# Second attention: TensorE instead of VectorE adds up head 1's exponentials, and the scores use two PSUM banks

## The reference

```python
xn = layernorm(x)
x = x + attention0(xn) + ternary_mlp(xn)      # 32 query heads, 8 key/value heads, rotary, causal
xn = layernorm(x)
x = x + gated_cumsum(xn) + attention1(xn)     # 16 heads of width 32, causal
```

```python
scores = einsum('bhtd,bhsd->bhts', Qf, Kf) / sqrt(32)
scores = where(causal, scores, finfo.min)
attn = softmax(scores, axis=-1)
out = einsum('bhts,bhsd->bhtd', attn, V)      # 16 heads
y = out.transpose(0, 2, 1, 3).reshape(B, T, 512) @ Wp
```

## Time and profile before

| | us |
|---|---|
| runs: median (lowest to highest) of 3 | 2744.94 (2737.44 to 2747.92) |
| profiled execution: span from first to last instruction | 2700.3 |
| PE busy, share of the span | 2390.0, 89% |
| PEld busy | 1489.7, 55% |
| DVE busy | 1759.7, 65% |
| ACT busy | 1250.1, 46% |
| POOL busy | 511.4, 19% |
| second attention: first exponential at, last at | 2008.9, 2596.2 |

### The profile page before, as it was taken

One profiled execution on the slowest core, in us unless ns is written; L12 is line 12 of the kernel. 1 busy time (PEld: TensorE's weight loads), 2 busy tenths in 40 slices (PEclk: granted clock), 3 DMA queues, 4 the chain that ended last, 5 costly groups with the idle time before them and its releaser, 6 DMA issues. The chain is left out here.

```text
span 2700.3 us, 42116 instructions
## 1 busy us (share of the span) xinstructions
PE 2390.0 (89%) x16373; PEld 1489.7 (55%) x16373; DVE 1759.7 (65%) x2057; ACT 1250.1 (46%) x2357; POOL 511.4 (19%) x447
## 2 busy tenths in 40 slices
PE   4959999959999999999999479979969999999947
PEld 2758888835444444444444457758745555555515
DVE  3745444537888888888880343422259999999954
ACT  2422222202777877877876121212215555556531
POOL 1110000010000000000000002220036676667650
PEclk8979999958999999999999789989979999999978
DMA  3771000060221221220000510015562222220024
GB/s 124 236 230 47 32 31 31 0 78 14 36 39 24 42 39 24 43 39 18 10 9 4 143 63 0 1 47 117 192 145 48 48 65 65 65 63 10 8 67 143
DMA packets 121390, 164.67 MB, mean 61 GB/s; under 512 B 60848, under 2 KB 66608, under 8 KB 115824
## 3 DMA queue, kind: packets, MB, share of 16 engines
q1 hardware_dynamic: 117744, 149.52, 22.8%
q10 hardware_dynamic: 3456, 12.58, 1.4%
HBM read 114.19 MB, written 47.71 MB: 60 GB/s over the span
## 5 line engine op out<-in xcount | busy, mean ns | idle before, releaser
L615 ACT ACTIVATE a_ex<-a_ps_s 128x512 f32<-128x512 f32 (+3 forms) x1280 | 622.8, 532 | 296.9 <-PE a_ps_s L670 220.4
L770 DVE TENSOR_REDUCE a_mx_part<-a_ps 128x2 f32<-128x1024 f32 (+3 forms) x576 | 585.8, 1043 | 132.5 <-PE a_ps L635 130.3
L1042 ACT ACTIVATE a_ex<-a_ps_s 128x512 f32<-128x512 f32 (+3 forms) x640 | 318.4, 532 | 286.1 <-PE a_ps_s L1103 159.8
L670 PE MATMUL a_ps_s<-a_q,a_k 50*128 50x512 f32 (+3 forms) x1152 | 399.8, 416 | 0.0
L635 PE MATMUL a_ps<-a_k,a_q 48*128 48x512 f32 (+3 forms) x1152 | 353.2, 419 | 33.0 <-DMA a_q<-q 29.2
L1017 POOL TENSOR_TENSOR a_acc<-a_acc,a_ex 128x512 f32<-128x512 f32 (+3 forms) x288 | 351.6, 1221 | 96.5 <-ACT a_ex L1042 75.6
L713 PE MATMUL a_ps_o<-a_ex,a_v 128*32 128x256 f32 (+1 forms) x5120 | 359.8, 363 | 5.9 <-ACT a_o L603 5.4
L1167 DVE TENSOR_REDUCE a_mx_part<-a_ps 128x2 f32<-128x1024 f32 (+2 forms) x320 | 336.3, 1054 | 34.6 <-PE a_ps L1069 22.8
L670 PEld LDWEIGHTS a_ps_s<-a_q,a_k 50*128 50x128 f32 x1152 | 182.8, 187 | 209.1 <-ACT a_ex L615 140.9
L1670 POOL TENSOR_TENSOR gc_z<-gc_state,gc_qg 128x512 f32<-128x512 f32 x16 | 26.3, 1641 | 1197.8 <-DVE gc_qg L1658 1197.8
L1066 PE MATMUL a_ps<-a_k,a_q 96*128 96x512 f32 (+3 forms) x640 | 212.6, 399 | 43.7 <-DMA a_q<-q 22.9
(11 more groups left out here) (202 smaller groups left out, 3894.7 us busy)
## 6 DMA issues: line engine op xcount, KB each, us to landing
a_q<-q SPq DMA_DIRECT2D x48, 256.0 KB, 5.4
a_k<-k SPq DMA_DIRECT2D x24, 512.0 KB, 4.9
a_q<-q SPq DMA_DIRECT2D x24, 512.0 KB, 6.9
q<-p_oh SPq DMA_DIRECT2D x32, 256.0 KB, 2.5
q<-p_ol SPq DMA_DIRECT2D x32, 256.0 KB, 2.8
w_o<-o SPq DMA_DIRECT2D x8, 1024.0 KB
w_z<-z SPq DMA_DIRECT2D x32, 256.0 KB
a_k<-k SPq DMA_DIRECT2D x48, 128.0 KB, 3.4
```

The costliest lines, as they stand in the source:

```text
L615: act.activation(ex[unit % NE][:, h % 2, off:CH], ps_s[n % 3][:, off:CH], ACT.Exp, scale=SCALE)\
L670: pe.matmul(ps_s[n % 3][:, off:CH], k_st[st][r0:r0 + KM, h % KH, t * P:(t + 1) * P], q_st[st][r0:r0 + KM, slot_h, c * CH + off:(c + 1) * C ...
L770: dve.tensor_reduce(mx_part[:, 2 * p:2 * p + 2, i, kc], bank[:, :, 0:w], AX.X, ALU.max).then_inc(taken1, 1)
L1042: act.activation(ex[s % NE][:, h, off:CH], ps_s[n % 3][:, off:CH], ACT.Exp, scale=SCALE)\
```

## The change

In the second attention VectorE no longer adds head 1's exponentials. TensorE does: `add_up(b, half)` takes a block of four steps and multiplies each step's head 1 tile with `first_one`, a 128x32 weight with ones in its first column. The four steps go to four column groups of 32, so their sums over the keys stand side by side in the bank `ps_z` (partitions 0, 32, 64 and 96), accumulated over a chunk's blocks. A block is done in two halves of 256 columns, in the even steps that follow it, behind `scores(s, 1)`. In a group's first chunk a 512-wide product with zeros opens the bank. At a chunk's end ScalarE copies the bank to `spread` (`take_spread`), and the product with ones in `sums` adds the four partial sums as it did the 128 partitions of `acc` before.

The bank for `ps_z` comes from the scores: they have two banks in place of three, one for each head, so `scores(s, h)` waits for the exponential of step s - 1 of its own head. The ring `ex` is released by GpSimd's additions, `times_v` and `add_up`. Head 0's way is as before. VectorE's memsets at the start are five instead of two, and TensorE waits for them.

Apart from this, `project0` gives its 38 semaphores back after `ternary_mlp`, and SyncE clears them at the start of `ternary_mlp`, ahead of its weight loads.

```diff
-        acc = [[sb(f"acc{i}_{n}", [P, CH]) for n in range(HG)] for i in range(2)]
-        one = sb("one", [P, DH])
+        acc = [sb(f"acc{i}", [P, CH]) for i in range(2)]
+        spread = [sb(f"spread{i}", [P, CH]) for i in range(2)]
+        one, first_one = sb("one", [P, DH]), sb("first_one", [P, DH])
+        zero = sb("zero", [P, CH], F32R)
...
-        ps_s = [psum(f"ps_s{i}", [P, CH]) for i in range(3)]
+        ps_s = [psum(f"ps_s{h}", [P, CH]) for h in range(HG)]
         ps_o = psum("ps_o", [P, CH])
+        ps_z = psum("ps_z", [P, CH])
...
+            def take_spread(g, c, s):
+
+                j = g * NCH + c
+                act.wait_ge(summed, 2 * (s // TPC + 1))
+                if j >= 2:
+                    act.wait_ge(scores1, SUMS_ENTRY[j - 2] + 1)
+                act.activation(spread[j % 2][:, :], ps_z[:, :], ACT.Copy).then_inc(spread_done, 1)
+
...
                     if h == 0 and s >= NE:
                         act.wait_ge(pv_done, (s - NE) // 2 + 1)
-                        act.wait_ge(added0, s - NE + 1)
-                        act.wait_ge(added1, s - NE + 1)
-                    act.activation(ex[s % NE][:, h, off:CH], ps_s[n % 3][:, off:CH], ACT.Exp, scale=SCALE)\
+                        act.wait_ge(added, s - NE + 1)
+                        act.wait_ge(summed, 2 * ((s - NE) // TPC + 1))
+                    act.activation(ex[s % NE][:, h, off:CH], ps_s[h][:, off:CH], ACT.Exp, scale=SCALE)\
                         .then_inc(exp_done, 1)
+                    if h == 0 and s - 4 in LAST_STEP:
+                        take_spread(*LAST_STEP[s - 4], s - 4)
...
-                pe.wait_ge(added0, s + 1)
-                pe.wait_ge(added1, s + 1)
-                for h in range(HG):
-                    mm = pe.matmul(ps_1[m % 2][h * DH:(h + 1) * DH, 0, :], one[:, :], acc[j % 2][h][:, :],
+                pe.wait_ge(added, s + 1)
+                pe.wait_ge(spread_done, j + 1)
+                for h, total in enumerate((acc[j % 2], spread[j % 2])):
+                    mm = pe.matmul(ps_1[m % 2][h * DH:(h + 1) * DH, 0, :], one[:, :], total[:, :],
                                    start=True, stop=True)
...
-                if n >= 3:
-                    pe.wait_ge(exp_done, n - 2)
+                if s > 0:
+                    pe.wait_ge(exp_done, n - HG + 1)
...
+            def add_up(b, half):
+
+                g, c, t0 = STEP_LIST[TPC * b]
+                pe.wait_ge(exp_done, TPC * (b + 1) * HG)
+                if t0 == 0 and half == 0:
+                    if b > 0:
+                        pe.wait_ge(spread_done, g * NCH + c)
+                    if c == 0:
+                        pe.matmul(ps_z[:, :], sel[:, 0, :], zero[:, :], start=True, stop=False)
+                for j in range(TPC):
+                    s = TPC * b + j
+                    off = max(first_col(c, t0 + j), half * CH // 2)
+                    cols = slice(off, (half + 1) * CH // 2)
+                    if cols.start < cols.stop:
+                        mm = pe.matmul(ps_z[j * DH:(j + 1) * DH, cols], first_one[:, :], ex[s % NE][:, 1, cols],
+                                       start=c > 0 and t0 == 0 and half == 0, stop=t0 == TPC * c and half == 1)
+                mm.then_inc(summed, 1)
+
...
             pe.wait_ge(blank, NS)
+            pe.wait_ge(part_init, 5)
...
                 if s % 2 == 1 and s > 1:
                     times_v(s // 2 - 1)
+                if s % TPC == 0 and s >= TPC:
+                    add_up(s // TPC - 1, 0)
+                if s % TPC == 2 and s > TPC:
+                    add_up(s // TPC - 1, 1)
             times_v(len(STEP_LIST) // 2 - 1)
+            for half in range(2):
+                add_up(len(STEP_LIST) // TPC - 1, half)
...
-                if 0 <= s - 2 < len(STEP_LIST):
-                    add_ex(s - 2)
...
         def _(sp):
+            for s in done_with:
+                sp.sem_clear(s)
```

More of the change, by code:

```diff
@@ L116, with project0 @@
 LN_SEMS = ("mean", "centred", "squared", "var", "root", "inverse", "scaled", "high", "low")
-def project0(nc, keep, A, X, xh, xl, ones_mean, eps, D):
+def project0(nc, keep, done_with, A, X, xh, xl, ones_mean, eps, D):
     with ExitStack() as ctx:
@@ L129, in sem @@
         def sem(n):
-            return keep.enter_context(nc.semaphore(f"p0_{n}"))
+            done_with.append(keep.enter_context(nc.semaphore(f"p0_{n}")))
+            return done_with[-1]
         COLS = QK0 + P
@@ L892, in attention_two @@
         scores2, exp_done, pv_done = sem("scores2"), sem("exp_done"), sem("pv_done")
-        added0, added1 = sem("added0"), sem("added1")
+        added, summed, spread_done = sem("added0"), sem("added1"), sem("spread_done")
         taken_o, staged = sem("taken_o"), sem("staged")
@@ L1008, in _ @@
                 j, off = g * NCH + c, first_col(c, t)
-                total, tile = acc[j % 2][0], ex[s % NE][:, 0, off:CH]
+                total, tile = acc[j % 2], ex[s % NE][:, 0, off:CH]
                 pool.wait_ge(exp_done, s * HG + 1)
@@ L1013, in _ @@
                         pool.wait_ge(scores1, SUMS_ENTRY[j - 2] + 1)
-                    pool.tensor_copy(total[:, :], tile).then_inc(added0, 1)
+                    pool.tensor_copy(total[:, :], tile).then_inc(added, 1)
                 else:
-                    pool.wait_ge(added0, s)
-                    pool.tensor_tensor(total[:, off:CH], total[:, off:CH], tile, ALU.add).then_inc(added0, 1)
+                    pool.wait_ge(added, s)
+                    pool.tensor_tensor(total[:, off:CH], total[:, off:CH], tile, ALU.add).then_inc(added, 1)
             join(GROUPS - 1, NCH - 1)
@@ L1047, in _ @@
                 take_o(GROUPS - 1, NCH - 1, len(STEP_LIST) // 2 - 1, odd)
+            take_spread(GROUPS - 1, NCH - 1, len(STEP_LIST) - 1)
         @block.tensor
@@ L1096, in scores @@
                 off = first_col(c, t)
-                if n >= 3:
-                    pe.wait_ge(exp_done, n - 2)
+                if s > 0:
+                    pe.wait_ge(exp_done, n - HG + 1)
                 diagonal = t >= TPC * c
-                mm = pe.matmul(ps_s[n % 3][:, off:CH], k_st[st][0:KM, h, t * P:(t + 1) * P],
+                mm = pe.matmul(ps_s[h][:, off:CH], k_st[st][0:KM, h, t * P:(t + 1) * P],
                                q_st[st][0:KM, h, c * CH + off:(c + 1) * CH], start=True, stop=not diagonal)
                 if diagonal:
-                    mm = pe.matmul(ps_s[n % 3][:, off:off + P], sel[:, 0, :], low_k[:, :], start=False, stop=True)
+                    mm = pe.matmul(ps_s[h][:, off:off + P], sel[:, 0, :], low_k[:, :], start=False, stop=True)
                 mm.then_inc(scores2, 1)
@@ L1158, in _ @@
             dve.memset(one[:, :], 1.0).then_inc(part_init, 1)
-            dve.wait_ge(part_init, 2)
+            dve.memset(first_one[:, :], 0.0).then_inc(part_init, 1)
+            dve.memset(zero[:, :].bitcast(F32), 0.0).then_inc(part_init, 1)
+            dve.wait_ge(part_init, 4)
+            dve.memset(first_one[:, 0:1], 1.0).then_inc(part_init, 1)
             def maxima(n):
@@ L1914, in build @@
             xl = inner.enter_context(nc.sbuf_tensor("xl0", [P, KT, TOK], F32R))
-            project0(nc, keep, A, X, xh, xl, ones_mean, eps, D)
-            ternary_mlp(nc, keep, A, X, xh, xl, ones_mean, D)
+            with ExitStack() as projecting:
+                done_with = []
+                project0(nc, projecting, done_with, A, X, xh, xl, ones_mean, eps, D)
+                ternary_mlp(nc, keep, done_with, A, X, xh, xl, ones_mean, D)
         attention(nc, shared, "a0", ATTN0, D, 0, neg_ident, masks[2])
```

14 lines of the change are left out of this document (1 added, 13 removed).

## The result

The changed kernel takes 2797.43 us (median of 4 runs; 2795.36 to 2862.66) against 2741.19 (2717.8 to 2747.92) of the kernel before on the same chip: ratio 1.0239 [1.0185, 1.0293]. The highest run, a disturbed one, is left out of the ratio. The two sets of medians differ by 56 and 65 us, so the change costs some 60 us, where the forecast had 33.

The account below looks back on a forecast made before the run. VectorE was the bound, TensorE close behind. Groups +40.7, with -3, -4 and +2.1, gave +36, less 3 made +33 us: 2733 on the 2700.3 us span, 2778 us with 44.6 up to the median; range 2742 to 2820.

Parts of the forecast that it names:

- groups at clock 1.00: Second attention: 296 steps, or 7.4 groups of 40 steps, each 5.5 us longer, +40.7 us.
- widths "rounded up": Diagonal steps of the second attention: product widths were said to be rounded up, so 3 us were taken off.
- granted clock: Second attention: a TensorE without gaps should keep 2.4 GHz, -4 us, chosen between 0 and -6.
- last 24 steps: Second attention's last steps: no maxima and room enough on TensorE, so no cost counted.
- end of the stage: Last sums of the second attention: less waiting for VectorE's additions, but two halves and a copy come in, -3 us.
- TensorE's own work before: Second attention, per group: 64.7 us summed from spacings, against 74.0 measured, leaving 9.3 us of room.
- 20 halves and the zero product: TensorE's added work per group: 20 x 0.66 us plus one 512-wide zero product of 0.23, 13.4 us.
- waits at a chunk's end: TensorE's value product waiting for ScalarE's output-bank copy, formerly partly in its room, now paid: 1.4 us a group.
- 0.1 us twice: TensorE in the second attention: 0.1 us each on the way into and out of the 32-column products.
- second rival: Two score banks bind: exponentials 0.25 us late in half of the steps, 37 us more, 2815 us; chance 0.20.
- Cheap halves: TensorE's halves cost only 0.40 to 0.46 us: +2 us, 2747 us, no change; chance 0.18.
- Real room in TensorE: Spacings hide TensorE idle time in the second attention: some 90 us less, 2655 us, half of that 2700; chance 0.12.

Follow-up runs that it names:

- e6: Kernel before with VectorE's additions for head 1 left out and nothing in their place, so head 1's sums are missing: 2683.72 us, ratio 0.9859.
- e3: Changed kernel with each half replaced by one 128-wide product, head 1's sums left out: 2721.64 us, ratio 1.0001.
- e5: Kernel before with only the change's two score banks, VectorE's additions kept: 2739.61 us against 2735.51.
- e1: The changed kernel run again without edit, beside the kernel before: 2784.35 us against 2718.91, ratio 1.0239.
- e4: Changed kernel with the halves moved behind the value products in the odd steps, bank copy one step later: 2786.62 us.
- e7: Changed kernel with one 512-wide sum per block of four steps in place of two halves: 2778.5 us, ratio 1.0226.
- e2: Kernel before with only the 38 semaphore clears ahead of the MLP's weight loads: 2734.25 us, ratio 0.9993.
- e8: Kernel before with the semaphore clears; GpSimd takes head 1's additions of each group's second chunk from VectorE: 2789.62 us.
- e9: Kernel before with the semaphore clears; GpSimd takes head 1's additions of each group's first chunk from VectorE: 2747.44 us, ratio 1.007.
- e10: Kernel before with the semaphore clears; GpSimd takes head 1's additions of every chunk's two narrowest steps from VectorE: 2746.11 us, ratio 1.0087.

## Why the prediction came out as it did

Direction and mechanism were right for the steady groups: VectorE stopped being the bound, TensorE's room was used up, and its column products set the step. The size was not. The measured 2797.43 us lies inside the wide range (2742 to 2820) and just above the forecast's own (2762 to 2795), and the cost was nearly twice the 33 us. By terms of the stage, in us:

| | predicted | measured |
|---|---|---|
| groups at clock 1.00 | 7.4 x 5.5 = +40.7 | 7.4 x 9.2 = +68 |
| widths "rounded up" | -3 | nothing: they were too small |
| granted clock | -4 | some -10 |
| last 24 steps | 0 | +6.5 |
| end of the stage | -3 | -4.5 |
| sum | +31 | +60 (stage: +59) |

The larger part lies in the first line, and there in one sum. For a group:

| | predicted | measured |
|---|---|---|
| TensorE's own work before | 64.7 | 68.5 (e6: 70.4 less 1.9 of waits) |
| 20 halves and the zero product | 13.4 | 20 x 0.77 + 0.2 = 15.6 |
| waits at a chunk's end | 1.4 | none that PE's gaps show |
| sum | 79.5 | 84.1; the group takes 83.3 |

*Own work, the step that failed.* "9.3 us of room" was 74.1 less 70.4, some 4. The 36.7 us of the twelve pairs off the diagonal rest on a stretch read directly; short were the terms that were scaled or counted. First, the diagonal's widths: with its mask a 384-wide product costs 0.04 us more than the prediction said and a 512-wide one behind a mask 0.05, and four passes (two heads, scores and maxima) in four chunks make 16 x 0.09 = 1.4 us. Second, the diagonal's 5.5 us a chunk has two value products, yet "0.1 us twice" once (2 x 1.87 + 0.99 + 0.55 + 0.2). The trace of after shows both paying on the way in and out there (0.16 us from a mask to L1136 instead of 0.06, and 0.22 for the 256-wide score behind it instead of 0.12), which is 0.2 us a chunk, 0.8 a group. Third, a flip was counted at its record of 0.38 us; with 0.1 us in, 0.31 and 0.1 us out it costs 0.51, 0.5 us a group. That is 2.7 of the 3.8 us; the rest was not found row by row and may hold short waits. The prediction then took off 3 us because its widths were "rounded up". They were too small, so that correction had the wrong sign.

*A half: 0.66 predicted, 0.77 measured.* The 0.56 us of the records and the 0.1 us on the way in were right. The 0.1 us behind it was missed, although show it: 0.35 us from the score after L1120 to the next product. The rule "0.1 us twice" was read off the value product and then applied once to the half. The Trainium skill, "TensorE: Matmul & The Clock Gate", section "Measured speedup vs the span model", gave an estimate of 0.40 us; the trace of after disagrees, as that of before had for the value product, with 0.56 us to the next start.

*The waits at a chunk's end* went the other way. Before, the value product's group was

```profile
L1120 PE MATMUL a_ps_o<-a_ex,a_v 128*32 128x512 f32 (+3 forms) x1280 | 158.7, 548 | 14.9 <-ACT a_o_odd L1031 14.9
```

and its 14.9 us of waiting became 0.2. In the changed kernel a half lies between, and the copy has ended when the value product comes; in e3, without the halves, 5.2 us of idle time are back. The prediction let the wait be "paid"; it was filled. This, and some 0.8 us that the sum can't place, is why the halves added 12.9 us to e6's 70.4 and not 15.6.

*The last 24 steps.* "Room enough" was wrong, and so was "it hides, at nothing" for the two banks there. Before, 47 exponentials took 32.2 us, after, 48 take 38.6, with PE busy 37.96 (windows of both kernels):

```profile
2565.40:2597.60 32.20, 29.77 (x175) 11.93 (x171) 30.50 (x30) 23.19 (x49) 29.62 (x22) 1.00 0.05 11
```

```profile
2656.80:2695.40 38.60, 37.96 (x264) 14.11 (x266) 2.21 (x7) 25.22 (x51) 28.43 (x26) 1.00 0.05 10
```

From start to start it is 31.6 and 38.1 us. PE has about 90 records more, but they are the smaller part of the 6.5 us. In the first eight of these steps the two banks alone (e5) bring 2.2 of the 2.6 us that the changed kernel loses, and e3, whose halves are gone, takes 38.4 us for all 24 (at clock 0.96). The prediction's cover for the banks counted "0.7 us of scores and maxima"; here there are no maxima. So its second rival, the score banks, was right for this piece of the stage.

*The clock.* The granted clock in the stage rose from 0.98 to 1.00, as predicted, and in e1, e4, e6 and e7, where TensorE is the bound too, it was 1.00 as well. But the term was too small. A mean of 0.98 between levels of 1.2 and 2.4 GHz stands for some 24 us at 1.2 GHz in 595, not 12. Two groups of before (start to start 76.9 and 78.1 us, where the others take 74.1) show the loss:

```profile
2228.00:2305.00 77.00, 72.60 (x410) 40.12 (x410) 73.59 (x102) 43.99 (x89) 51.22 (x45) 0.96 0.24 57
...
2379.00:2457.00 78.00, 73.75 (x409) 40.79 (x409) 72.94 (x100) 43.93 (x88) 51.15 (x45) 0.93 0.24 56
```

That is 6.8 us, and 3.0 more lie in the first 16 steps of the last group (33.5 us at clock 0.90, where other groups take 30.5): some 10 us. It was not this one execution alone: the mean clock of the stage was 0.96 to 0.99 in e2, e5, e8, e9 and e10 too, where VectorE still does most of head 1's additions. Why it falls there was not tested.

*End of the stage.* From the start of the last exponential to the end of the last sums it was 9.0 us and is 4.5: -4.5 where -3 was said.

So errors cancelled in part, and that is luck and not foresight: the clock and the end gave back some 7 us more than was forecast, without which the stage would have been further off.

*The marks set for the profile.* The half stood as said (0.56 and 0.33 us), TensorE hardly waits for maxima, the MLP stage starts 2 us later. The stage is 656 us where 620 to 635 were said (the prediction's own +31 gives 626), and the step 2.08 where 1.98 was. VectorE is busy 362 us in it and not 311: before, its records added up to 626 us in 575 us of busy time, so some 50 us of them overlapped, and the 264.6 us of the removed groups were more than they had added to its busy time. Of no effect here, as VectorE is off the path.

*Clears:* +2.2 us for +2.1. *GpSimd's additions:* priced at nothing and off the path, they fell by 36 us, and in e6, where VectorE's additions are gone and nothing else, they fell to the same 316.0.

*The base.* The prediction called the 44.6 us between span and median "launch and end". For the profiled execution after, device time and span are both known: 2795.36 and 2793.6, 1.8 us apart. The 44.6 us fit another granted clock in other executions: the profiled one of before had a mean of 0.940, and runs of this kernel with 0.941 take 2698.49 and 2699.41 us. This did no harm to the sum, since the difference was added to the median; but it would have if a term had been scaled to the span.

*The rivals.* Cheap halves: refuted, 0.56 us to the next start. Real room in TensorE: refuted by e6, which stops at 70.4 us a group with no additions left on VectorE. The rule from "Best Practices" in the Trainium skill's "Trainium Kernel Development and Optimization", which names the share of peak FLOPs beside the weight loads, speaks of the distance to the roofline; the prediction read it as idle time. In e6 PEld is busy 77.31 of 140 us, about half, and still the group stops at 70.4 us. The score banks: right for the last 24 steps, as said. In the groups e3 shows no loss by them (some 70.1 us without its small products, against the 70.4 of e6 with three banks), but e5 does by 1.2 us and e4 by its late scores, where no column product stands in the even step; e7 points the same way. The halves cover the very wait that a cheaper arrangement of them would lay open.

## What to carry to other kernels

Before work goes from the bound engine to the next one, take the work out of the bound engine without putting it anywhere (here e6): one run gives the real room, 4 us a group instead of the 9 that came from summed-up spacings. Such a run is not a working kernel, only a measurement. A group of column products costs its records plus a change of form on both sides, so one that is put between other products pays about 0.2 us extra each time. And two savings may share one cover: here the halves hid the smaller number of score banks, so making them shorter or moving them gave back little (1.1 and 0.6 us a group). A cover has to be looked for in every stretch: at the stage's end, with no maxima between the scores, the two banks cost 2.2 us in eight steps.

## What the runs showed of the hardware

- The granted clock of a long, steadily busy stage differs between executions of the same code. In the first attention the same products took windows of 890 us at clock 0.98 and 930 at 0.92, and in e8 the window that holds them took 990 us at 0.86:

```profile
600.00:1590.00 990.00, 960.05 (x9136) 461.44 (x9134) 686.33 (x761) 638.95 (x1312) 0.00 (x0) 0.86 0.14 24
```

  VectorE's busy time is nearly the same in all three (679.12, 681.71 and 686.33 us). The runs of the kernel before go the same way: the fastest, 2691.49 us, had a mean clock of 0.946, the slowest, 2816.93, one of 0.893.
- GpSimd's additions have a mean of 1096 ns where VectorE does not add beside them (1097 in e6), and 1221 where it does (1220 in e2): 11% more beside the neighbour, on the same 288 instructions.
- The change between full-width products and four-column products cost 0.1 us in and 0.1 us at the second product after, for each group of them, whether it was 256 or 512 wide (e7).
